# Shared feed-forward work moved into the gaps of one PSUM bank during a state-space scan

## The reference

```
x = x + layernorm(mamba(layernorm(x)))      # a state-space scan, D_INNER 512, D_STATE 16
x = x + layernorm(ffn(layernorm(x)))        # shared + routed feed-forward
```

## Time and profile before

| | us |
|---|---|
| median of 3 runs (1503.97 to 1511.75) | 1506.67 |
| the profiled execution, its own time | 1497.41 |
| span from its first to its last instruction | 1495.6 |
| PE busy, share of the span | 1187.9, 79% |
| DVE busy | 1020.1, 68% |
| POOL busy | 1016.0, 68% |
| ACT busy | 802.4, 54% |
| mean granted TensorE clock | 0.904 of full |

### The profile page before, as it was taken

One profiled execution on the slowest core, in us unless ns is written; L12 is line 12 of the kernel. 1 busy time (PEld: TensorE's weight loads), 2 busy tenths in 40 slices (PEclk: granted clock), 3 DMA queues, 4 the chain that ended last, 5 costly groups with the idle time before them and its releaser, 6 DMA issues.

```text
span 1495.6 us, 15504 instructions
## 1 busy us (share of the span) xinstructions
PE 1187.9 (79%) x4766; PEld 523.0 (35%) x4767; DVE 1020.1 (68%) x1059; ACT 802.4 (54%) x1387; POOL 1016.0 (68%) x476
## 2 busy tenths in 40 slices
PE   4775868879878787797887877974999999999940
PEld 2221223224223222331332322423455656666620
DVE  4697998898998989899899897871311123322237
ACT  6666568658668677677766865554111111111137
POOL 0599999999999999999999999990363000000035
PEclk9897899999899899899889988996999999999975
DMA  3801301220230240240150131021954011111135
GB/s 103 320 0 58 119 23 58 98 85 31 89 123 2 99 142 2 76 164 1 58 169 1 59 127 56 1 71 56 370 202 151 0 39 42 44 47 42 39 116 179
DMA packets 78243, 129.54 MB, mean 87 GB/s; under 512 B 7648, under 2 KB 56416, under 8 KB 74080
## 3 DMA queue, kind: packets, MB, share of 16 engines
q1 hardware_dynamic: 68624, 112.07, 22.1%
q0 software_dynamic: 3072, 8.39, 1.7%
q10 hardware_dynamic: 6480, 8.26, 1.6%
HBM read 96.46 MB, written 32.24 MB: 86 GB/s over the span
## 4 chain that ended last, share of the span: by engine, by line
PE 35%; POOL 33%; issue 13%; DVE 11%; ACT 7%; DMA 1%; POOLq 0%; DVEq 0%; ACTq 0%
POOL state L513 19%; POOL bx L502 10%; PE psX L1606 10%; PE psX L1555 6%; DVE state L1092 5%; PE bank L1623 2%; PE psY L1623 2%; PE psY L1497 2%; POOL fy L579 2%; PE psY L1576 2%; PE bank L1576 2%; PE bank L1419 2%; DVE acc L1027 2%; POOL lt L518 1%; PE bank L1454 1%
## 5 line engine op out<-in xcount | busy, mean ns | idle before, releaser
L513 POOL TENSOR_TENSOR state<-state,cbc 128x1024 f32<-128x1024 f32 x256 | 606.2, 2390 | 11.2 <-DVE state L1092 11.0
L1092 DVE TENSOR_TENSOR_SCAN state<-psX,bx 128x1024 f32<-128x1024 f32 x256 | 577.5, 2278 | 38.0 <-ACT psX L742 23.9
L742 ACT ACTIVATE psX<-dt,aneg 128x511 f32<-128x511 f32 x512 | 330.5, 678 | 205.4 <-DVE state L1092 203.7
L502 POOL TENSOR_TENSOR bx<-xh,bbc 128x1024 f32<-128x1024 f32 x128 | 309.5, 2418 | 58.8 <-DMA bbc<-bc_rows 42.0
L1497 PE MATMUL psY<-state,ident 64*64 64x512 f32 x2048 | 293.9, 664 | 27.1 <-POOL state L513 26.8
L1454 PE MATMUL bank<-prow,ident 128*128 128x512 f32 x256 | 166.5, 737 | 114.1 <-DVE bx L1080 113.9
L579 POOL DMA_INDIRECT fy<-slot_out,slot x32 | 33.2, 1037 | 316.6 <-DMA slot_out<-yo 307.1
L1080 DVE TENSOR_TENSOR bx<-xh,bank 128x1024 f32<-128x1024 f32 x128 | 152.9, 1195 | 7.9 <-PE bank L1454 7.8
L1497 PEld LDWEIGHTS psY<-state,ident 64*64 64x64 f32 x2048 | 63.5, 142 | 218.2 <-issue 134.4
L1244 DVE TENSOR_TENSOR actN<-sg,psX 128x512 f32<-128x512 f32 x39 | 26.8, 687 | 141.3 <-ACT sg L930 141.3
L1454 PEld LDWEIGHTS bank<-prow,ident 128*128 128x128 f32 x256 | 47.3, 219 | 204.5 <-DVE bx L1080 168.0
(11 more groups left out here) (193 smaller groups left out, 1547.3 us busy)
## 6 DMA issues: line engine op xcount, KB each, us to landing
cbc<-bc_rows SPq DMA_DIRECT2D x32, 1024.0 KB, 5.0
bbc<-bc_rows SPq DMA_DIRECT2D x16, 1024.0 KB, 6.2
slot_in<-ao SPq DMA_DIRECT2D x1, 4992.0 KB, 27.4
xsl<-slot_in SPq DMA_DIRECT2D x39, 128.0 KB, 2.2
slot_out<-yo ACTq DMA_DIRECT2D x39, 128.0 KB, 2.4
xin<-in_x SPq DMA_DIRECT2D x8, 512.0 KB, 4.4
xr<-in_x SPq DMA_DIRECT2D x8, 512.0 KB, 5.4
x_rows<-ao SPq DMA_DIRECT2D x8, 512.0 KB, 2.9
```

Of the source, the lines that this page charges most:

```text
L502: nc.gpsimd.tensor_tensor(bx[q % RB][:], xh[par][:, h * CH:(h + 1) * CH], bbc[:, n // 2].unsqueeze(1).broadcast_to([P, CH, L]), ALU.mult). ...
L513: nc.gpsimd.tensor_tensor(w[:], w[:], cbc[:, n].unsqueeze(1).broadcast_to([P, CH, L]), ALU.mult).then_inc(weighted, 1)
L742: e = nc.scalar.activation(decay[q % RD][:, c, 1:L], dt[par][:, h * CH + c, 1:L], ACT.Exp, scale=aneg[:, h * CH + c, n:n + 1])
L1092: nc.vector.tensor_tensor_scan(st[q % RS][:].rearrange("p c t -> p (c t)"), decay[q % RD].rearrange("p c t -> p (c t)"), bx[q % RB][:].rea ...
```

## The change

Twelve gaps are opened in psB during each of the batches 2 to 5, for the shared feed-forward of batch e = i - 2, which is still in the columns buffer xnTb. After odd steps 1, 3, 5, 7 (gate), 13, 15, 17, 19 (up) and 21, 23, 25, 27 (down) PE puts one chunk into psB, and only in the following step, when ACT or DVE has taken it out, the next `spread_b`. ACT takes out gate and down chunks as the first thing of its step, ahead of the decays; DVE multiplies the up chunks in. A silu of 4x512 is added on ACT in step 10. Batch 5 takes the place of batch 0 in the last scanning batch, straight from xnTb. The groups left for the shared stage are 4, 6 and 7.

Further parts: the inject of step 12 goes from POOL to DVE (`BY_POOL`); PE's output projections of steps 15 and 17 come ahead of that step's `total`; ACT copies the B and C rows ahead of Abs; `cbc` shrinks to 8 rows and `load_c` to eight loads a batch; the multiplication of rows by score goes from POOL to DVE (`scale_rows`) with a buffer for every batch, and all eight loads stand ahead of the weights; the shared results go through DRAM for five batches and come back as two loads, behind the residual of the first half.

```diff
+    BY_POOL = [q % 2 == 0 and q not in (12,) for q in range(Q)]
+    EARLY_AT = (1, 3, 5, 7, 13, 15, 17, 19, 21, 23, 25, 27)
-    LATE = NB - 1
+    LAST = NB - 3
+    LATE_B = (NB - 4, NB - 2, NB - 1)
+    LATE = len(LATE_B)
-        cbc = sb("cbc", [P, N, L], where=A)
+        cbc = sb("cbc", [P, 2 * CG, L], where=A)
+        sga = sb("sga", [P, FC, L], where=A)
+        ystage = sb("ystage", [P, J, DIM], where=A)
-        xrow = [fx0[:, i * J:(i + 1) * J] for i in range(2)]
+        xrow = [(fx0, ysh)[b // (NB // 2)][:, b % (NB // 2) * J:(b % (NB // 2) + 1) * J] for b in range(NB)]
...
# SP
+            def load_c(f, k):
+                g, slot = k % CS, k % 2
+                if not (isinstance(f, int) and f == 0 and k < 2):
+                    sp.wait_ge(weighted, Q * f + CG * (k - 1))
...
+                if do_scan and 2 <= i <= NB - 3:
+                    e = i - 2
+                    sp.wait_ge(e_kept, J * (e + 1))
+                    sp.dma_start(pick(yshb_v, e), ystage[:]).then_inc(e_stored, 16)
...
+            for b in range(NB):
+                sp.dma_start(xrow[b], xnb_v[b]).then_inc(xrow_loaded[b], 16)
...
-            sp.wait_ge(e_stored, 16)
-            sp.dma_start(ysh[:, 0:J, :], ysh_d).then_inc(ysh_loaded, 16)
             load_residual(fx0, 0)
+            sp.wait_ge(e_stored, 16 * (NB - 4))
+            sp.dma_start(ysh[:, 0:LATE_B[0] * J, :], ysht_v[:, 0:LATE_B[0] * J, :]).then_inc(ysh_loaded, 16)
+            sp.wait_ge(l_stored, 16)
+            sp.dma_start(ysh[:, LAST * J:(LAST + 1) * J, :], yshb_v[LAST]).then_inc(ysh_loaded, 16)
# POOL
-                    if q % 2 == 0:
+                    if BY_POOL[(q + RB) % Q]:
                         if q + RB < Q:
                             inject(i, par, q + RB)
...
-                nc.gpsimd.tensor_tensor(xrow[b % 2], xrow[b % 2],
-                                        score[:, b * J:(b + 1) * J].unsqueeze(2).broadcast_to([P, J, DIM]),
-                                        ALU.mult).then_inc(xrow_scaled, 1)
# ACT
                 if q == 14:
+                    act.wait_ge(proj_ready, f + 1)
+                    nc.scalar.activation(prow[par][:], psF[:], ACT.Identity).then_inc(prow_kept, 1)
                     act.wait_ge(z_done, f + 1)
                     nc.scalar.activation(tmp[:], acc[:], ACT.Abs).then_inc(sf, 1)
-                    act.wait_ge(proj_ready, f + 1)
-                    nc.scalar.activation(prow[par][:], psF[:], ACT.Identity).then_inc(prow_kept, 1)
...
+            def early(e, q):
+                if q in (1, 3, 5, 7):
+                    c = q // 2
+                    act.wait_ge(e_gate, FC * e + c + 1)
+                    nc.scalar.activation(sga[:, c], psB[:], ACT.Identity).then_inc(e_gate_kept, 1)
+                if q in (21, 23, 25, 27):
+                    j = (q - 21) // 2
+                    act.wait_ge(e_down, J * e + j + 1)
+                    if j == 0 and not (isinstance(e, int) and e == 0):
+                        act.wait_ge(e_stored, 16 * e)
+                    nc.scalar.activation(ystage[:, j], psB[:, 0:DIM], ACT.Identity).then_inc(e_kept, 1)
...
                 for q in range(Q):
+                    if do_early:
+                        early(i - 2, q)
                     if q + RD < Q:
                         if do_scan:
                             decays(i, par, q + RD)
...
+                    if do_early and q == 10:
+                        early_silu(i - 2)
# DVE
+            def early_act(e, c):
+                dve.wait_ge(e_silu, e + 1)
+                dve.wait_ge(e_up, FC * e + c + 1)
+                nc.vector.tensor_tensor(sga[:, c], psB[:], sga[:, c], ALU.mult).then_inc(e_act, 1)
...
                         scan(i, q)
-                        if q % 2 == 0:
+                        if q + 1 < Q and not BY_POOL[q + 1]:
                             inject(i, par, q + 1)
+                    if do_early and q in (13, 15, 17, 19):
+                        early_act(i - 2, (q - 13) // 2)
...
+            scale_rows(0)
             for u in range(2, LATE * FC):
+                if u - 1 < NB:
+                    scale_rows(u - 1)
                 sh_act(u // FC, u // FC % 2, u % FC)
# PE
                 for q in range(Q):
-                    if q % 2 == 1:
+                    do_early = do_scan and 2 <= i <= NB - 3
+                    if do_early and q in EARLY_AT:
+                        pe.wait_ge(dve_bx, i * DQ + NTH_D[q + 1])
+                        early(i - 2, q)
+                    elif do_early and q - 1 in EARLY_AT:
+                        early_taken(i - 2, q - 1)
+                        spread_b(i, par, q + 1)
+                    elif not BY_POOL[(q + 2) % Q]:
                         if q + 2 < Q:
                             if do_scan:
                                 spread_b(i, par, q + 2)
...
+                    if do_back and q in (15, 17):
+                        back(i - 1, q, do_front)
                     if do_scan and q >= SUM_LAG:
                         total(i, par, q - SUM_LAG)
```

More of the change, by code:

```diff
@@ L39, in build @@
     PN = N // 2
-    PQ = H * PN
+    BY_POOL = [q % 2 == 0 and q not in (12,) for q in range(Q)]
+    PQ = sum(BY_POOL)
     DQ = Q - PQ
+    NTH_P = [sum(BY_POOL[:q]) for q in range(Q + 1)]
+    NTH_D = [q - sum(BY_POOL[:q]) for q in range(Q + 1)]
     RD = 2
@@ L208, in build @@
         b_loaded = [sem(f"b_loaded{i}") for i in range(PN // CG)]
-        c_loaded = [sem(f"c_loaded{i}") for i in range(N // CG)]
-        rows_stored = sem("rows_stored")
-        e_loaded = sem("early_columns_loaded")
+        c_loaded = [sem(f"c_loaded{i}") for i in range(2)]
         e_gate = sem("early_gate_ready")
@@ L220, in build @@
         ysh_loaded = sem("ysh_loaded")
+        l_gate = sem("last_gate_ready")
+        l_gate_kept = sem("last_gate_kept")
+        l_silu = sem("last_silu")
+        l_up = sem("last_up_ready")
+        l_act = sem("last_act")
+        l_down = sem("last_down_ready")
+        l_kept = sem("last_kept")
+        l_stored = sem("last_stored")
+        rows_stored = sem("rows_stored")
         decay_ready = sem("decay_ready")
@@ L279, in build @@
         ex_ready = sem("ex_ready")
-        xrow_loaded = [sem(f"xrow_loaded{i}") for i in range(2)]
+        xrow_loaded = [sem(f"xrow_loaded{i}") for i in range(NB)]
         xrow_scaled = sem("xrow_scaled")
@@ L380, in iteration @@
                 if do_scan:
-                    load_c(i, par, 3)
+                    for k in range(1, 5):
+                        load_c(i, k)
                 if do_front:
@@ L384, in iteration @@
                     sp.dma_start(rows(f).rearrange("a r t -> (a r) t"), prow[1 - par][0:2 * N]).then_inc(rows_stored, 16)
+                if do_scan:
+                    load_c(i, 5)
+                if do_front:
                     load_b(f, 1 - par, 0)
-                    load_c(f, 1 - par, 0)
+                if do_scan:
+                    load_c(i, 6)
+                    load_c(i, 7)
                 if do_back:
@@ L390, in iteration @@
                 if do_front:
-                    load_c(f, 1 - par, 1)
+                    load_b(f, 1 - par, 1)
                 if do_back:
@@ L760, in iteration @@
                         back(i - 1, q)
+                    if do_early and q == 10:
+                        early_silu(i - 2)
                     if not do_front:
-                        early(q)
+                        last(q)
                     if q == 10 and (do_front or do_back):
@@ L1524, in iteration @@
                     else:
-                        early(q)
-                    if do_back:
+                        last(q)
+                    if do_back and q not in (15, 17):
                         back(i - 1, q, do_front)
```

171 lines of the change are left out of this document (97 added, 74 removed).

## The result

Measured beside the kernel before, the changed kernel needs 1485.85 us (median of 4; before 1506.81): ratio 0.9859, 95% interval 0.9832 to 0.9887. In a second measurement the same two kernels read 1472.9 and 1498.2: 0.9826, 0.9797 to 0.9855. So it is faster, by 21 and by 25 us (1.4 and 1.7%); 38 were forecast, and the time lies inside the range.

The account below looks back on a forecast made before the run. DVE with what feeds it and POOL were both taken as limits of a batch, POOL alone in the last. From 1497.4 us, -82.5 + 38 + 1.2 - 2.4 + 2.4 + 5 gave 1459 profiled, 1468 as median; range 1438 to 1497.

Parts of the forecast that it names:

- third slot tile: Early in the routed stage PE waits for slot 2, queued on SP behind other loads: +5 us, bounds 0 and 13.
- The walk: A middle batch followed step by step: 9.5 us late at scan 21, +38 for four batches.
- gate gaps: Steps 1 to 8: a gap's 4.4 us hides behind other work; 0.5 us expected only in steps 1 to 3.
- I take 0 and bound it by 4: Down gaps, steps 21 to 31: no cost expected, at most 4 us for two chunks and two copies.
- The detour: From scan 20 through POOL and ACT to DVE's L1041: 11.4 us, as long as before, covering chunks 21 and 23.
- the second spread of step 11 and the sum behind it: PE's spread and total after DVE's inject of step 12: 2.0 us, then the dt product starts 3.5 later.
- Product 12: Inject of step 12, now on DVE: step 11's spread waits for it and the dt product ends 2.7 us late.
- 17 + 7 us: PE's added work in a middle batch, said to fit into its 24 idle us only on average.
- Gaps hidden: Rival for batches 2 to 5: only DVE's own 3.9 us a batch count, 16 instead of 38; 1446 us, chance 0.22.
- psB in series: Rival for batches 2 to 5: every gap costs its full 2.4 us, 29 a batch; 1546 us, chance 0.08.
- End stage bound: Rival: eight products delay POOL's issues by 7.4 us; scatter costs +4, slot 2 +8; 1480 us, chance 0.20.
- Median: Whole kernel: the median of 1506.7 us stands 9.3 above the profiled time, so 1459 became a forecast of 1468.

Follow-up runs that it names:

- before again: The kernel before, unchanged, profiled a second time, on the side where it needs about 1500 us: 1499.5 us.
- changed again: The changed kernel, unchanged, measured and profiled a second time, beside a kernel before of 1498.2 us: 1472.9 us.
- no_down: The changed kernel without the four down gaps (steps 21 to 27 of batches 2 to 5) and ACT's four copies: 1472.6 us, 130.8 per batch.
- pool12: The changed kernel with product 12 of every batch back on POOL, the gaps kept: 1477.0 us.

## Why the prediction was right, and where it was too high

Against the two profiles without the stalls (before again 1497.4, changed again 1471.9, span each), term by term:

```
                                   predicted   measured
up to the end of batch 1             +0.6        -3.1
batches 2 to 5                      +38.0       +56.0
batch 6                              +0.6        -0.5
batch 7                              -2.4        -1.9
scans' end to shared stage            0          -1.3
shared stage, with scale_rows       -80.1       -80.0
third slot tile                      +5          +5.6
finish                                0          -0.3
sum                                 -38.3       -25.5
```

- *Shared stage.* Four groups of 20.6 us went, as worked out from the earlier trace rows. `scale_rows` was to give 2.4 back as a wait of PE. The wait grew by 1.2 us only, and the gate and up matmuls behind it took 5.2 us, from start to start, in place of 3.5. Before again, then changed again:

```profile
1067.92 1.95 PE L1555 MATMUL psX<-xg,shg 128*128 128x512 f32 x4 [1.74 <-DVE actS L1201]
```

```profile
1118.06 2.81 PE L1644 MATMUL psX<-xg,shg 128*128 128x512 f32 x4 [2.92 <-DVE actS L1243]
```

  So the agreement to 0.1 us is partly luck.
- *Batches 2 to 5: the mechanism right, the size low.* 9.5 us each was forecast, 14.0 came. The walk held in its order: gate gaps 0 (0.5 forecast), scan 19 late by 10.7 and scan 24 by 11.1 in batch 5, where scan 21 was to be 9.5 late. Two terms were mis-sized. The first: **"I take 0 and bound it by 4"**, for the down gaps; no_down shows 2.6. The detour covered chunks 21 and 23, but PE already had no slack beside the four sums, and I had looked only at whether ACT waits for them. The second makes up the remaining 1.9 us and lies in steps 11 to 14: the B and C rows were to start 3.8 us late and started 5.7 late (60.2 us behind scan 0 against 54.5, batch 5). The walk gave the second spread of step 11 and the sum behind it 2.0 us together; they took 3.6 in most batches. The batches of changed again differ in just this. PE in batches 2 and 3 (granted clock 0.98 from 344 to 350 us, 0.64 from 477 to 487):

```profile
344.68 1.12 PE L1506 MATMUL bank<-prow,ident 128*128 128x512 f32 x2 [1.03 <-DVE bx L1120]
...
346.76 3.70 PE L1433 MATMUL bank<-xh,xp 128*128 128x512 f32 x8
```

```profile
477.78 2.08 PE L1506 MATMUL bank<-prow,ident 128*128 128x512 f32 x2 [1.03 <-DVE bx L1120]
...
481.70 4.89 PE L1433 MATMUL bank<-xh,xp 128*128 128x512 f32 x8
```

  With a fast second spread the way from scan 11 to 14 took 12.8 us, with a slow one 14.3 (batches 4 and 5), with a slow dt product as well 15.8. So PE at the low clock costs 1.5 us there in most batches, most of the 1.9. Scan 11 itself came 1.0 us later than in the kernel before, in the mean of the four. The first spread doesn't count: it took 2.07 us in the kernel before too.
- *Product 12.* The walk had it as 2.7 us of lateness in step 11; pool12 measured 3.3. Moved by itself it did not relieve what bounds the batch: the earlier trace rows showed POOL nearly full, and the rows behind them DVE and PE as the limit. Batches 0 and 1, which I took as 0 and 0.6, read 124.5 and 120.8 us against 128.9 and 117.7 in this pair of profiles; but the first profile of the same changed kernel has 129.5 and 117.9, so the -3.1 of the table is a difference between profiles and not the change's.
- *Batch 7*: POOL's, 2.3 us from the loss to the last weighing for one product of 2.4.
- *PE's load.* "17 + 7 us" doesn't follow from its terms: eight chunks of 1.8 are 14. PE got 20 us more. Nothing in the sum hangs on it. The waits of POOL for `cbc`, put at nothing, didn't come.
- *Third slot tile.* +5 forecast from SP's queue and the bytes, 5.66 measured on the 1498 side; on the other a stall of ACT took its place.
- *The rivals.* "Gaps hidden" is out: 14 us a batch, not 4. "psB in series", 29, is out as a whole; it is what happens in the up gaps alone, 10.2 for four, 2.5 each, by the price the prediction gave it (2.4). "End stage bound": the delay of POOL's issues is there (below), about 3.4 us in all where 7.4 were priced, and it was hidden. In changed again the scatter's last issue ended at 1161.3 and PE's last down half at 1168.2.
- *Median.* The forecast added the 9.3 us by which the kernel before stood above its profile. That difference was probably the one between the two sides: the profile agrees with the 1498 side, the times shown are of the 1506 side. The changed kernel differs by 13 between the two.

## What to carry to other kernels

Before work is put into the gaps of a resource, write down the engine's load step by step and not per batch: here PE was 80% busy in the mean, with two stretches (35 us around the projection, 20 around the sums) in which added work made the batch longer, and two (steps 1 to 8 and 20 to 24) in which the chunks put there cost nothing or under a microsecond. The same chunks cost 0, 1 or 2.5 us each by where they stood; moving them, with product 12 back on POOL, brought 1485.9 to 1460.6. Moving work off the busiest engine helps only if that engine ends the wait: look at who waits for whom beside the busy share.

## What the runs showed of the hardware

*PE's clock after a short rest.* In the changed kernel again, windows of 10, 11, 5 and 34 us from step 7 on (granted clock in the third column from the end):

```profile
590.00:600.00 10.00, 8.81 (x36) 2.27 (x34) 9.74 (x7) 6.24 (x12) 9.35 (x5) 1.00 0.17 64
600.00:611.00 11.00, 4.30 (x11) 1.11 (x12) 10.70 (x18) 7.73 (x8) 8.43 (x4) 0.66 0.09 37
611.00:616.00 5.00, 5.00 (x14) 1.36 (x14) 3.92 (x3) 4.97 (x6) 3.77 (x3) 0.72 0.60 210
616.00:650.00 34.00, 33.41 (x150) 14.95 (x148) 23.77 (x25) 20.13 (x25) 23.25 (x11) 1.00 0.22 65
```

PE is idle for more than half of the second window (5.9 us of it in one piece) and the granted clock falls to the level of 1.2 GHz for part of it; it is back at 2.4 GHz during the third, and the instructions in between take nearly twice as long. The last row is the full stretch: 33.41 busy of 34. The kernel before rests at the same place and shows the same slow spread (before again):

```profile
699.15 2.07 PE L1454 MATMUL bank<-prow,ident 128*128 128x512 f32 x2 [4.99 <-DVE bx L1080]
```

What the low clock costs in a batch stands in the account of batches 2 to 5 above.

*DVE's products of two SBUF inputs and POOL's issues.* `scale_rows` on DVE (L1276, 1.22 us at 1128.13) runs beside the scatter's issues. POOL, same kernel:

```profile
1127.07 0.97 POOL L585 DMA_INDIRECT slot_in<-fx,slot  x1 [0.30 <-issue]
1128.34 1.85 POOL L585 DMA_INDIRECT slot_in<-fx,slot  x1 [0.30 <-issue]
1130.49 0.97 POOL L585 DMA_INDIRECT slot_in<-fx,slot  x1 [0.30 <-issue]
```

Three of the 32 issues took 1.85 us in place of 0.97, at 1128.34, 1131.77 and 1135.21, each begun 0.2 us after such a product: 0.9 us each, as the inject in the earlier trace rows. Beside the other products the delays were smaller (1.23 and 1.42 us) or none (0.97 for an issue begun before the product, at 1124.48). The Trainium skill, page "SBUF — State Buffer", section "SBUF: two separate sides", gives the lock between such a product and a GpSimd operation that reads SBUF. The rows fit it, with the issue of an indirect transfer as the GpSimd operation; no run takes the products away to prove it.

*Two sides.* Where the kernel before reads 1506 us, every profile of a changed kernel (seven) has ACT idle for 9.2 to 12.0 us in the shared stage and DVE and ACT idle in the finish, with no releaser in the records:

```profile
1458.52 0.75 DVE L1331 BATCH_NORM_STATS2 fst<-fy 128x6 f32<-128x256 f32 x2 [5.57 <-issue]
```

The finish, from the first gather to the end, is 60.7 to 61.7 us there and 52.5 to 53.3 where the kernel before reads 1498 to 1500; there none of six profiles has such a wait. The kernel before was not profiled on the 1506 side; that its 8 us more there are the same stalls is likely and not shown. What causes them no run here tells, nor whether it is a trait of the chip: by the numbers of the chips in the record, 10 stands on the 1506 side, 13 on the 1498 side, and 7 on both (1500.05 us and, 16 minutes later, 1506.23). For a comparison it means that two profiles may be set against each other only if the kernel before ran equally fast beside both.
